# Attention and sparse FFN in float32 on one core: product banks, rounds and the order of late work rearranged

## The reference, cut

```python
def reference(x, qkv, o_proj, gamma, beta, w_gate, w_up, w_down):   # x (1, 2048, 512)
    xn = layernorm(x)
    xh = layernorm(xn) * gamma + beta
    q, k, v = xh @ qkv[:, :512], xh @ qkv[:, 512:1024], xh @ qkv[:, 1024:]
    attn = softmax(causal(q @ k.T / sqrt(512))) @ v
    h = silu(xn @ w_gate) * (xn @ w_up)          # (2048, 2048)
    h = keep_two_of_four_by_magnitude(h)
    return x + (attn @ o_proj + xn) + h @ w_down
```

## Time and profile before

| | |
|---|---|
| median of 3 runs | 833.1 us (831.1 to 834.9) |
| the profiled execution | 830.72 us, of it span 828.9 us |
| granted TensorE clock, mean | 0.998 of full |
| busy: PE / DVE / ACT | 809.8 / 583.1 / 303.8 us |

### The profile page before, as it was taken

How to read it: one execution, slowest core, us unless ns; L and a number is a source line. 1 busy time by engine, 2 the same in 40 slices (tenths; PEclk the granted TensorE clock), 3 DMA queues, 4 the chain that set the end, 5 groups by cost and what they waited for, 6 DMA issues and landing times.

```text
span 828.9 us, 9550 instructions
## 1 busy us (share of the span) xinstructions
PE 809.8 (98%) x3643; PEld 660.8 (80%) x3643; DVE 583.1 (70%) x1002; ACT 303.8 (37%) x498; POOL 13.5 (2%) x33
## 2 busy tenths in 40 slices
PE   8999999999999999999999999998999999999997
PEld 5788787888888888887778778887888888888875
DVE  6867776546532448769789789699568567667796
ACT  6333123112311225564535435364234333423531
POOL 2010101000000000000000000000000000000000
PEclk9999999999999999999999999999999999999999
DMA  9431442030201026565444454771467153161002
GB/s 324 158 116 51 141 139 77 26 128 26 76 19 59 26 97 284 196 261 215 178 183 146 179 206 158 320 280 66 162 219 259 80 228 134 44 229 51 1 0 102
DMA packets 30013, 117.04 MB, mean 141 GB/s; under 512 B 2912, under 2 KB 2960, under 8 KB 27536
## 3 DMA queue, kind: packets, MB, share of 16 engines
q1 hardware_dynamic: 25792, 108.83, 35.2%
q10 hardware_dynamic: 4176, 7.60, 2.8%
HBM read 74.45 MB, written 41.97 MB: 140 GB/s over the span
## 4 chain that ended last, share of the span: by engine, by line
PE 73%; DVE 11%; ACT 5%; issue 3%; DVEq 0%
PE bank L488 10%; PE bank L490 9%; PE bank L489 9%; PE bank L646 9%; PE bank L647 9%; PE bank L648 9%; PE bank L728 5%; PE bank L730 5%; PE bank L729 5%; ACT mag L842 3%; PE bank L530 2%; DVE hs_lo L1193 2%; PE bank L546 1%; DVE wset L958 1%; DVE g_sum L1134 1%
## 5 line engine op out<-in xcount | busy, mean ns | idle before, releaser
L646 PE MATMUL bank<-X_hi,wset 128*128 128x512 f32 x448 | 175.9, 393 | 3.5 <-DVE g_sum L1134 2.9
L647 PE MATMUL bank<-X_lo,wset 128*128 128x512 f32 x448 | 174.5, 389 | 0.0
L648 PE MATMUL bank<-X_hi,wset 128*128 128x512 f32 x448 | 174.3, 389 | 0.0
L646 PEld LDWEIGHTS bank<-X_hi,wset 128*128 128x128 f32 x448 | 84.1, 188 | 26.7 <-ACT bank L838 5.6
L648 PEld LDWEIGHTS bank<-X_hi,wset 128*128 128x128 f32 x448 | 84.1, 188 | 17.5
L647 PEld LDWEIGHTS bank<-X_lo,wset 128*128 128x128 f32 x448 | 84.1, 188 | 16.9
L728 PE MATMUL bank<-dw,hs_hi 128*128 128x512 f32 x224 | 88.0, 393 | 2.1 <-DVE acc L1158 1.7
L729 PE MATMUL bank<-dw,hs_hi 128*128 128x512 f32 x224 | 87.2, 389 | 0.0
L730 PE MATMUL bank<-dw,hs_lo 128*128 128x512 f32 x224 | 87.2, 389 | 0.0
L1158 DVE TENSOR_TENSOR acc<-bank,acc 128x512 f32<-128x512 f32 x64 | 43.4, 687 | 49.5 <-PE bank L730 49.5
L488 PE MATMUL bank<-xT_hi,zg_hi 128*128 128x512 f32 (+3 forms) x160 | 58.8, 367 | 0.0
(11 more groups left out here) (173 smaller groups left out, 1381.7 us busy)
## 6 DMA issues: line engine op xcount, KB each, us to landing
w_operands<-wset SPq DMA_DIRECT2D x8, 3584.0 KB, 11.9
wset<-w_operands SPq DMA_DIRECT2D x8, 3584.0 KB, 11.5
wsum<-w_units SPq DMA_DIRECT2D x28, 256.0 KB, 3.5
dw_raw<-L_ffn_w_down SPq DMA_DIRECT2D x14, 512.0 KB, 4.8
xw<-L_attn_x SPq DMA_DIRECT2D x4, 1024.0 KB, 9.5
xt_raw<-x_t SPq DMA_DIRECT2D x8, 512.0 KB, 7.5
xn_t<-xt_raw SPq DMA_DIRECT2D x8, 512.0 KB, 4.5
X_raw<-xn_t SPq DMA_DIRECT2D x8, 512.0 KB, 4.8
```

The lines of the kernel that those rows point to most:

```text
L646: pe.matmul(dst[:], u[:, 0, :], x_hi, start=(first and kt == 0), stop=False, skip_group_check=True)
L647: pe.matmul(dst[:], u[:, 0, :], x_lo, start=False, stop=False, skip_group_check=True)
L648: last = pe.matmul(dst[:], u[:, 1, :], x_hi, start=False, stop=(kt == 1), skip_group_check=True)
```

## The change

1. Start. The four "vo_weight" products get banks 4 to 7 of their own (`product_bank`), so that the z products of chunk 0 in banks 0 to 3 follow only the "qk_weight" ones. The last round of the first weight product runs by thirds (hi·hi, lo·hi, hi·lo for all four), as the others do. All four wide rows of chunk 0 are copied to SBUF by ACT. Steps are reordered: `xh` of a quarter with its z round, `*vo` (the evictions) behind them, statistics of chunk 1 partly behind `z[0]`, `("x_turn", 0, 1)` behind the first scores.
2. `x_scale[2]` stands ahead of `v[1][2]`.
3. z of chunks 2 and 3 is made in rounds.
4. Block 2: `sums(3)` moves behind the first add of `down`, the weight parts behind the second.
5. The second pass's T operands: T1, T2 and T3 are formed in block 7 ahead of and behind the adds of P7, from loads into regions of their own (`b12_apart`, `b22_apart`, `t1_apart`), T4 behind the first add of `down`. SP issues `load_made(8)` and `store_set(7)` later.
6. End: the choice of half 13 starts a block earlier (`mag_apart`), its low parts are made ahead of block 15's adds; halves 13 and 14 accumulate in the same four banks (6, 7, 2, 3), so four adds fall away; `down(14)` runs by hidden rows over all four banks, `down(15)` in two pairs of tiles; DVE's last block sums stand ahead of the choice of half 14.

```diff
-              hi[2][0], hi[3][0], lo[2][0], lo[3][0], vo_round[0], hi[2][1], qk[0], hi[3][1], *qk[1:4], lo[2][1], lo[3][1], vo_round[1],
-              xw_load[2], xt_load[1], hi[2][2], hi[3][2], hi[2][3], hi[3][3], x_scale[0], ("x_rows", 0, 0), ("x_turn", 0, 0),
-              lo[2][2], lo[3][2], vo_round[2], lo[2][3], lo[3][3], vo_round[3], *xh_pre[0][0:2], xh[0][0], z_round[0][0],
-              *vo, xh[0][1], z_round[0][1], xh_pre[0][2], xh[0][2], z_round[0][2], xh_pre[0][3], xh[0][3], z_round[0][3],
-              ("x_rows", 0, 1), *stat[1], x_stats[1], x_rstd[1], xw_load[3], *z[0], ("x_turn", 0, 1), v[0][0], x_scale[1],
-              ("scores", 0, 0), exp[0], row_turn[1], row_store[1], row_spread[1], v[0][1]]
+              hi[2][0], hi[3][0], lo[2][0], lo[3][0], vo_round[0], hi[2][1], qk[0], hi[3][1], qk[1], lo[2][1], lo[3][1], vo_round[1],
+              xw_load[2], xt_load[1], hi[2][2], hi[3][2], x_scale[0], ("x_rows", 0, 0), lo[2][2], lo[3][2], *qk[2:4], hi[2][3], hi[3][3],
+              ("x_turn", 0, 0), vo_round[2], lo[2][3], lo[3][3], vo_round[3]]
+    steps += [step for k in range(KT) for step in (xh_pre[0][k], xh[0][k], z_round[0][k])]
+    steps += [*vo, *stat[1][0:2], *z[0], *stat[1][2:4], x_stats[1], x_rstd[1], xw_load[3], ("x_rows", 0, 1), v[0][0],
+              ("scores", 0, 0), exp[0], ("x_turn", 0, 1), x_scale[1], v[0][1], row_turn[1], row_store[1], row_spread[1]]
     before = {3: [z_round[1][0]]}
     between = {3: [z_round[1][1], xh_pre[1][3], xh[1][2], z_round[1][2], xh[1][3], z_round[1][3], *z[1], xn[1][0], v[1][0], xn[1][1],
                    xn_store[1], xt_load[2]],
-               7: [z[2][0], *stat[3], x_stats[3], x_rstd[3], xt_load[3], *z[2][1:4], v[2][0]],
-               11: [z[3][0], xn[3][0], z[3][1], xn[3][1], xn_store[3], *z[3][2:4], v[3][0]]}
+               7: [z_round[2][0], xh_pre[2][3], z_round[2][1], xh[2][3], z_round[2][2], *stat[3], z_round[2][3], x_stats[3], x_rstd[3],
+                   xt_load[3], *z[2], v[2][0]],
+               11: [*z_round[3], *xn[3], xn_store[3], *z[3], v[3][0]]}
     beside = {0: [v[0][2], xh_pre[1][0]],
               1: [xh_pre[1][1], v[0][3], xh[1][0]],
               2: [xh_pre[1][2], xh[1][1]],
               3: [*stat[2], x_stats[2], x_rstd[2], v[1][1]],
-              4: [v[1][2], x_scale[2], row_turn[2], row_store[2], *xn[0], row_spread[2], xn_store[0]],
-              5: [v[1][3], *xh_pre[2][0:2], xh[2][0]],
-              6: [xh_pre[2][2], xh[2][1], xh_pre[2][3], *xh[2][2:4]],
+              4: [x_scale[2], v[1][2], row_turn[2], row_store[2], *xn[0], row_spread[2], xn_store[0]],
+              5: [v[1][3], xh_pre[2][0], xh[2][0]],
+              6: [xh_pre[2][1], xh[2][1], xh_pre[2][2], xh[2][2]],
...
-        row_bank = [bank[6], bank[7], bank[4], bank[5]]
+        row_bank = [bank[6], bank[7], bank[0], bank[1]]
+
+        def product_bank(no):
+
+            return bank[no] if KT <= no < 2 * KT else prod_bank[no % PROD_RING]
+
+        def products_ahead(no):
+
+            return 0 if no < 2 * KT else no - 2 * KT + 1 if no < 3 * KT else no - PROD_RING + 1
...
-            return bank[((6, 7, 2, 3), (0, 1, 4, 5), (6, 7, 2, 3))[i - (ND - 3)][t] if i >= ND - 3 else 6 + (TC * i + t) % 2]
+            return bank[((6, 7, 2, 3), (6, 7, 2, 3), (0, 1, 4, 5))[i - (ND - 3)][t] if i >= ND - 3 else 6 + (TC * i + t) % 2]
...
-                sp.wait_ge(set_stored[q % 2], 16 * (q // 2 + 1))
+                sp.wait_ge(set_stored[q % 2], 16 * (NQ // 2))
...
-                    load_X(1, B11, 0, 2)
-                    sp.wait_ge(full[1], FILLS * n + F_P7)
-                    load_X(1, T3, 0, 3)
+                    load_X(X_raw[B11], X_loaded[B11], 0, 2)
+                    load_X(b12_apart, b12_loaded, 0, 3)
+                    sp.wait_ge(full[1], FILLS * n + F_P2)
+                    load_X(X_raw[B21], X_loaded[B21], 2, 2)
+                    sp.wait_ge(full[1], FILLS * n + F_P6)
+                    load_X(b22_apart, b22_loaded, 2, 3)
+                    load_made(n + 1)
                     sp.wait_ge(full[1], FILLS * n + F_P3)
-                    load_X(1, B22, 2, 3)
-                    load_X(1, B21, 2, 2)
-                if n + 2 < N_Q:
+                    load_X(X_raw[B22], X_loaded[B22], 2, 3)
+                    store_set(n)
+                if n + 2 < N_Q and n != NQ - 2:
                     sp.wait_ge(full[1], FILLS * (n + 1))
                     if n + 2 < NQ:
                         sp.wait_ge(set_stored[n % 2], 16 * (n // 2 + 1))
                         load_set(n + 2)
                     else:
                         load_made(n + 2)
-                if n + 1 < NQ:
+                if n + 1 < NQ - 1:
...
-                if q == KT - 1:
-                    pe.wait_ge(w_ready[left], q + 1)
-                    pe.wait_ge(w_ready[right], q + 1)
-                    whole_parts(of, 0, q, lhs, rhs)
-                    return
                 for m in range(KT):
                     part(of, 0, m, q, lhs, 0, rhs, 0)
                 pe.wait_ge(w_ready[left], q + 1)
@@ -570,12 +590,16 @@
                     part(of, 0, m, q, lhs, 1, rhs, 0)
                 pe.wait_ge(w_ready[right], q + 1)
                 for m in range(KT):
-                    part(of, 0, m, q, lhs, 0, rhs, 1)
+                    last = part(of, 0, m, q, lhs, 0, rhs, 1)
+                    if q == KT - 1:
+                        last.then_inc(prod_full, 1)
...
+                if n == q == 0:
+                    pe.wait_ge(rows_kept, 2)
...
+            def down_part(i, t, r):
+
+                s_hi, s_lo = hs_hi_at(i)[:, r, t * P:(t + 1) * P], hs_lo_at(i)[r][:, t * P:(t + 1) * P]
+                d_h, d_l = dw_at(i // 2)[:, r // 2, 0, r % 2, :], dw_at(i // 2)[:, r // 2, 1, r % 2, :]
+                dst = down_bank(i, t)[:]
+                pe.matmul(dst, s_hi, d_h, start=(r == 0 and i != ND - 2), stop=False)
+                pe.matmul(dst, s_hi, d_l, start=False, stop=False)
+                last = pe.matmul(dst, s_lo, d_h, start=False, stop=(r == G - 1 and i != ND - 3))
+                if r == G - 1:
+                    last.then_inc(down_full, 1)
...
+            def down_by_hidden(i, some):
+
+                for t in some:
+                    bank_free(i, t)
+                for r in range(G):
+                    if 0 in some:
+                        hidden_wait(i, r)
+                    for t in some:
+                        down_part(i, t, r)

             for n in range(N_Q + 2):
                 if n < N_Q:
                     gate_up(n)
                 if n == 1:
                     pe.wait_ge(rows_ready, NT)
-                if n >= 2:
+                if 2 <= n < N_Q:
                     down(n - 2)
+                elif n == N_Q:
+                    down_by_hidden(ND - 2, range(TC))
+                elif n > N_Q:
+                    down_by_hidden(ND - 1, (0, 1))
+                    down_by_hidden(ND - 1, (2, 3))
...
+                elif kind == "x_turn":
+                    act.wait_ge(rows_turned, 2 * k + 2)
+                    for row in (2, 3) if k == 0 else (0, 1):
                         nc.scalar.copy(spread[0][:, row, :], row_bank[row][:]).then_inc(rows_kept, 1)
...
+                if n == N_Q - 2:
+
+                    act.wait_ge(full[1], FILLS * (n + 1))
+                    for r in range(G):
+                        magnitude(ND - 3, r)
...
-                elif n <= 2:
+                elif n == 1:
                     sums(n + 1)
                 if n == 1:
                     for m in range(4):
@@ -1222,9 +1303,16 @@
                 if n >= 4 and n % 2 == 0:
                     down_lo(n // 2 - 1)
                 elif n == N_Q - 1:
+                    for r in range(G):
+                        kept_lo(i, r)
                     down_lo(ND // 2 - 1)
+                if n == NQ - 1:
+                    second_T1()
+                    second_T2()
                 add_sum(0, n, bank[4], F_P7, g_sum[2], 3)
                 add_sum(1, n, bank[5], F_P7, b_tile(n, 1), 3)
+                if n == NQ - 1:
+                    second_T3()
...
-                    X_first(1)
                     add_down(i, 0)
-                    X_second(1)
-                    X_third(1)
+                    second_T4()
+                    X_lo_half(1, 0)
                     add_down(i, 1)
-                    X_fourth(1)
-                    dve.wait_ge(X_summed, 8)
-                    X_lo_half(1, 0)
-                    add_down(i, 2)
                     X_lo_half(1, 1)
                     X_lo_half(1, 2)
+                    add_down(i, 2)
+                    for o in range(3, NOP - 1):
+                        X_lo_half(1, o)
                     add_down(i, 3)
-                    for o in range(3, NOP):
-                        X_lo_half(1, o)
+                    X_lo_half(1, NOP - 1)
+                elif n == 2:
+                    add_down(i, 0)
+                    sums(n + 1)
```

(19 more changed lines are left out.)

265 lines of the change are left out of this document (139 added, 126 removed).

## The result

The median fell from 832.8 us (4 runs, 831.1 to 834.9) to 825.3 us (4 runs, 824.6 to 826.0): ratio 0.991, 95% interval 0.988 to 0.993. The forecast was 820.8, with 816 to 826 as its range. The direction held, and the range with 0.7 us to spare; of the 12.15 us expected, some 7.5 to 8 came.

What follows compares the result with a forecast made beforehand. PE bounds the kernel (busy 809.8 of 828.9 us), so only its waits can be filled. Terms −1.65 (parts 1 and 2), −1.65, −2.95, −0.4, −5.5 make −12.15: 833.1 to 820.95, stated as 820.8, range 816 to 826.

Steps and rivals of the forecast that it cites:

- Parts 2, 3, 4, 6: Chunk 2's early scale −2.0 us, z of chunks 2 and 3 in rounds −1.65, block 2 −2.95, the end −5.5.
- the sum: Whole kernel: all terms add to −12.15 us, from 830.72 to 818.6 profiled, or from 833.1 to 820.95 as median.
- the slow clock behind the wait: At down(15), nine matmuls at about half clock behind the 2.71 us wait would run at full clock: −1.73 us.
- running down(14) by hidden rows: At the end, down(14) would run without its waits for single low parts: −0.75 us.
- Part 5: Between the passes, blocks 7 to 8: −0.4 us, bounds −2.2 and +3, with w_down delayed 0 to 3.
- Its own sign of being wrong: A gap of several us at block 8 or 9 with a load or `dw` as releaser would refute the prediction.
- The rival: Between the passes, w_down or a set lands late and DVE's queue holds block 8's P7 adds: +2 to +3, chance 0.2.
- The new stall at P2: At P2 of block 8, PE waits for the seed copy behind T3's high part: 1.0 to 1.3 us.
- the wait at block 8's P7 sums: PE's wait of 2.1 us there should shorten; among the signs it was to stay near 2.
- Part 1: At the start, a lead of 2.9 us is lost again to a later spread; z of chunk 1 0.35 later.

Runs made afterwards that it cites:

- w_down first: Changed kernel, but SP issues the w_down load ahead of the load of block 9's weight set that waits for a store: 818.8 us, ratio 0.983.
- store early: Changed kernel, but the store of block 7's weight set is issued at the start of block 7, ahead of the token loads: 818.8 us, ratio 0.983.
- passes undone: Changed kernel with the second pass's T operands made behind block 7 again, loads and stores as before the change: 820.0 us, ratio 0.984.
- the nine: Nine profiles of kernels sharing the changed first stage, the changed kernel among them: z of chunk 1 begins at 67.93 to 70.14 us.
- both: Changed kernel with w_down first, plus chunk 1's statistics in chunk 0's quarters, and scale, turn and copy ahead of the first scores: 815.2 us, ratio 0.978.

## Why the forecast was right, and where not

**What bounds the kernel, and that it would be faster:** right. No matmul was added, and each gap that was to go went.

**Parts 2, 3, 4, 6** were sized within 0.2 in the trace (−3.7, −2.9, −5.7), and undoing them cost 1.7, 1.8, 2.1 and 4.9 in the medians, where 2.0, 1.65, 2.95 and 5.5 had been forecast. In part 6 the sum's reason was half right: the slow clock behind the wait, 1.7 of the 5.5, is not always there, and running down(14) by hidden rows, for which I counted 0.75, is worth 0.2.

**Part 5 is the step that failed.** The forecast saw the chain (late store, the set's load behind it, w_down behind both) and gave it 0 to 3 us and a chance of 0.2. Its own sign of being wrong came: a gap of several us at block 8, released by ACT, which had waited for `dw_raw`. Three of its numbers were off, all to the same side. It took 12 for the store; it ran 16.1, with the load of block 8's set (12.6) and a token load beside it at first, and 11.0 where it ran ahead of them. Even in the kernel before, this store had taken 14.4. It let the data land at 562 to 567 in the time of the kernel before; they landed at 565.2, which in that time is 569.9, since PE was 4.7 ahead by then: 2.9 past the late end, most of it the 4.1 that the store took longer. And it measured the delay at DVE's queue, where w_down is wanted at 569.5; ACT's queue wants it at 562.9, and behind ACT's first cast stands the copy that P5 waits for. ACT has 1.6 of idle behind the two casts in the kernel before; what was beyond that went to PE: 6.07 of ACT's wait became 4.3 of gap, and the clock fell behind it, another 2.4, which the sum had at nothing. The rival's +2 to +3 was too low by 2.7, for the step came out 5.7 above the forecast (+5.3 for −0.4). The computing side of part 5 was right in kind: it gains 1.3 (forecast 0.4). The new stall at P2 came as forecast, 1.03 from start to start for 1.0 to 1.3, but the wait at block 8's P7 sums, which was to stay near 2, shrank to 0.1 with w_down first. That the median still lies in the range is luck in part. The sum was made against one profiled execution; there it gave 818.6, and 825.98 was measured, 7.4 more. The median is only 4.5 over, since the profile of the kernel before was its shortest execution and that of the changed kernel its longest.

The Trainium skill's rule ("DMA: Bandwidth & Descriptors", Queues, rings and completion order) that descriptors of one queue and engine start in order agrees with the runs: 12.8 us for w_down behind a 3.5 MB load, and 5.9, 4.6 and 4.5 without one, with w_down first, store early and passes undone.

**Part 1:** the mechanism was right (the copy behind a second `v_lo`, forecast 49.9, measured 50.21; v at 40.8, measured 41.0), the size short by 1.5 in this profile, by 0.2 to 2.4 in the nine. The spread took 5.8 where 4.8 was put in, and the idle of 2 us that it made was followed by slow matmuls, which the sum had not priced. The forecast gave the clock a price at the end of the program only.

**The median and the profile.** Profile against profile the change is −4.7, by medians −7.5. The runs of the kernel before that were made beside the experiments show why: of 28 times, the seven with a mean clock of 0.998 lie at 831.1 to 832.4, ten at 0.996 at 832.5 to 834.4, and the rest, at 0.993 to 0.995, at 833.2 to 835.4. Its profiled execution has 0.998, and a time below all 28. The changed kernel's profile has 0.993 and the longest time of its four, which reach down to 824.6 at 0.998. So two extremes of the clock were compared. So the gaps of 2 us in the kernel before, which show full clock behind them in its profile (1.85 and 1.64 in the earlier trace rows, 2.08 at block 8's P7 sums), are in other executions probably followed by slow stretches; that is inferred from the mean clocks, since only one execution was traced. The window behind the last of them:

```profile
570.00:575.00 5.00, 2.92 (x14) 2.13 (x13) 5.00 (x8) 1.55 (x4) 0.00 (x0) 1.00 0.00 0
```

It is in line with it that the kernels without long gaps, w_down first and both, have a clock of 0.999 to 1.000 in all eight runs and spread by 1.3 and 0.7 us; of the four runs of store early, three have 1.000 and the fourth 0.998 and 821.0, 1.8 above the next.

## What to carry to other kernels

A queue entry that waits holds everything behind it: when a load is made to wait for a store, look at what is queued behind that load, and follow the late data to the engine queue that asks for it first, not to the one with the heavier work. A lead on the critical path is worth only what the next shared resource lets through: here 2.9 us were won in the first 40, and lost again because the next chunk's statistics and one small copy behind them came 2 us later in the same edit; with both moved forward 2.0 to 2.4 of it stayed. Fill an engine's known idle slot (0.8 us per quarter) rather than the head of its next burst.
